# Layer 0 of a four-layer kernel: scores in two pairs of PSUM banks, weights normalised before they are turned, products on halved columns, one routing chain, broadcast norm factors

## The reference, cut to what matters

```
q, k, v = x @ wq.T (16 heads of 64), x @ wk.T, x @ wv.T (4 kv heads of 64)
q, k = rmsnorm(q), rmsnorm(k)
scores = q k^T / 8, masked to a causal window of 64
y = softmax(scores) @ v;  out = y @ wo.T
# beside it: layernorm, a small attention over the 4 batches, layernorm,
# router -> softmax -> top 2 of 8 experts, experts w1, gelu, w2
```

## Time and profile before

| | |
|---|---|
| median of three runs | 1451.62 us (1449.86, 1451.62, 1457.27) |
| the profiled execution, its own time | 1449.79 us |
| its span | 1448.0 us |
| mean granted TensorE clock | 0.926 of 2.4 GHz |
| busy, share of span: TensorE, VectorE, ScalarE, GpSimd | 89%, 63%, 46%, 21% |
| scores steps | 32, their maxima from 82.4 to 555.5 us |
| first GpSimd scatter of layer 0, of layer 1 | 182.80 us, 594.48 us |
| first exponential of layer 1 | 646.63 us |

### The profile page before, as it was taken

The page is one execution under the profiler, slowest core; times in us unless marked ns, Lnnn a source line. Parts: engine busy times, 40 slices in busy tenths (PEclk is TensorE's granted clock), DMA queues, the critical chain, the costliest instruction groups (busy, mean ns, idle before and its releaser), DMA issues.

```text
span 1448.0 us, 23894 instructions
## 1 busy us (share of the span) xinstructions
PE 1291.5 (89%) x9334; PEld 791.3 (55%) x9334; DVE 913.3 (63%) x1975; ACT 664.0 (46%) x1424; POOL 302.3 (21%) x309
## 2 busy tenths in 40 slices
PE   6878697997997888779899979999799989899998
PEld 4456565876674666445666757755344323224555
DVE  4478753343354568865687657677578868775366
ACT  2345042762651322016443535566466646576621
POOL 1242072000102510474001201044421312101000
PEclk8988698998998879759999989999999989999999
DMA  8000023332100220123523463321330121200000
GB/s 247 21 1 1 1 85 120 89 106 70 29 8 18 57 39 4 62 66 71 144 85 99 123 163 105 121 69 30 66 74 4 33 39 34 36 1 29 1 8 22
DMA packets 65101, 86.23 MB, mean 60 GB/s; under 512 B 9566, under 2 KB 49374, under 8 KB 63326
## 3 DMA queue, kind: packets, MB, share of 16 engines
q1 hardware_dynamic: 60892, 76.30, 20.1%
q0 software_dynamic: 4096, 8.40, 2.0%
HBM read 62.19 MB, written 22.48 MB: 58 GB/s over the span
## 4 chain that ended last, share of the span: by engine, by line
PE 63%; DVE 13%; DMA 9%; POOL 5%; issue 4%; ACT 3%; SPq 3%; DVEq 0%; ACTq 0%; POOLq 0%
PE psB L420 29%; PE psA L420 27%; PE psB L424 5%; DMA wA<-slots_x 3%; DVE mx L1478 2%; POOL slots_x L1945 2%; DMA arena<-scr1k 2%; PE psA L424 2%; DMA arena<-scr2k 2%; DVE st L1177 1%; ACT pbuf L1807 1%; ACT pbuf L1725 1%; DMA arena<-slots_x 1%; SPq L2049 1%; DMA scr1k<-arena 1%
## 5 line engine op out<-in xcount | busy, mean ns | idle before, releaser
L1807 ACT ACTIVATE pbuf<-psA 128x512 f32<-128x512 f32 (+3 forms) x768 | 350.6, 489 | 249.0 <-PE psA L420 241.1
L1478 DVE TENSOR_REDUCE mx<-psA 128x1 f32<-128x512 f32 (+3 forms) x520 | 326.0, 660 | 83.5 <-PE psA L420 80.7
L420 PE MATMUL psA<-arena 64*64 64x128 f32 (+6 forms) x1504 | 187.9, 291 | 2.2 <-ACT pbuf L1807 1.4
L420 PEld LDWEIGHTS psA<-arena 64*64 64x64 f32 (+3 forms) x1504 | 111.1, 135 | 70.4 <-ACT pbuf L1807 30.6
L1725 ACT ACTIVATE pbuf<-psA,st,rq 128x128 f32<-128x128 f32 x256 | 92.7, 467 | 99.9 <-DVE st L1181 99.9
L420 PE MATMUL psA<-arena,w 96*128 96x512 bf16 (+4 forms) x320 | 112.7, 404 | 6.1 <-DMA arena<-scr2k 3.3
L420 PE MATMUL psA<-w_mdiagT,w_identb 128*128 128x128 bf16 x512 | 108.8, 222 | 0.0
L420 PE MATMUL psB<-pbuf,arena 128*5 128x512 f32 (+3 forms) x1024 | 93.4, 438 | 0.5 <-ACT pbuf L1807 0.4
L420 PE MATMUL psB<-xf,wA 128*128 128x128 f32 x624 | 93.0, 294 | 0.0
L1904 POOL TENSOR_TENSOR sm<-sm,w_ohalf 128x4 f32<-128x4 f32 x24 | 24.5, 1030 | 294.7 <-DVE sm L1048 294.7
L420 PEld LDWEIGHTS psB<-xf,wA 128*128 128x128 f32 x624 | 81.5, 203 | 7.6 <-issue 2.4
(11 more groups left out here) (318 smaller groups left out, 2325.5 us busy)
## 6 DMA issues: line engine op xcount, KB each, us to landing
wA<-in_moe SPq DMA_DIRECT2D x39, 576.0 KB, 3.8
wA<-in_moe SPq DMA_DIRECT2D x39, 256.0 KB, 3.1
slots_x<-wA SPq DMA_DIRECT2D x20, 256.0 KB, 3.7
slots_y<-tH SPq DMA_DIRECT2D x18, 256.0 KB, 3.7
wA<-slots_x SPq DMA_DIRECT2D x15, 256.0 KB, 4.0
arena<-scr2k SPq DMA_DIRECT2D x48, 64.0 KB
scr1q<-arena SPq DMA_DIRECT2D x4, 384.0 KB, 3.9
scr1k<-arena SPq DMA_DIRECT2D x4, 384.0 KB, 4.2
```

The costliest lines, as they stand in the source:

```text
L420: return pe.matmul(out, lhsT, rhs, start=start, stop=stop, skip_group_check=True)
L1478: dv.tensor_reduce(m[:, t, h:h + c], maxb(lay, b, n)("mx", lay, b, n)[:, 0:c * k].rearrange("p (c k) -> p c k", c=c), AX.X, ALU.max) \
L1807: ac.activation(pb(lay, b, s, j)[:, 0:T - q0_], scoreb("ex", lay, b, s, j)[:, 0:T - q0_], ACT.Exp, bias=0.0, scale=1.0) \
```

## The change

- The scores alternate between two pairs of banks (psA0 and psA1). bT and outP go; turned tiles of both x and the products use accO alone, in turn. The output projection, and the first batch's ks0, rq0, kn0, use misc.
- The exponentials also give their row sums (accum_out). A new VectorE part nz inverts them and multiplies the weights in SBUF (128x512 per x) before they are turned. The column of ones goes.
- The products take v as the stationary side (64 columns, the left or right half of the output partitions) and the turned weights of both x as the moving side (128 columns), so their result is already turned; the four turns go, and the copy of yt is one plain copy. The heads' order in wo0 follows.
- ln3 and kn0 turn a broadcast view of the factors; the widening copies go.
- rt of layers 0 and 1 is a copy of the logits per batch; a new step rts does softmax and comparisons for all four batches at once, in instructions of 128x1024.
- MERGE is written anew. In it, layer 0's routing stands before the first batch's sixth scores step (before: its seventh), the scatter steps still before the second batch's ks0, and the fourth batch's k0, ks0 and kn0 among the third batch's steps (before: behind them), so that they also stand ahead of the second gather as they did.

The diff, cut to its core (MERGE, renamed signals and lines that only follow are left out):

```diff
-        both = Ring([A[0][:, :, :]])
+        both = Ring([a[:, :, :] for a in A])
         scoreb = Ring([A[0][:, k, :] for k in range(2)])
-        bT = Ring([A[1][:, 1, :]])
-        outP = Ring([A[1][:, 0, :]])
...
-        PTs = Ring([v.rearrange("p (k c) -> p k c", k=4) for v in ptiles[4:7]])
-        ysb = Ring([ptiles[7].rearrange("p (k x d) -> p k x d", k=4, x=2)])
+        PTs = Ring([pbuf[:, i, :, :].rearrange("p x (k c) -> p x k c", k=4) for i in (2, 3)])
...
-                pe.wait_ge(*ln_wide.at(tag, b))
-                v, bank = tA("wide", tag, b).rearrange("p (t r) -> p t r", t=4), misc(*u)
-                tr4(bank, lambda t: v[:, t, :]).then_inc(*ln_turned.up(tag, b))
-                tA.give(("wide", tag, b), ln_turned.now())
+                pe.wait_ge(*ln_pow.at(tag, b))
+                st, bank = small("ln", tag, b), misc(*u)
+                tr4(bank, lambda t: st[:, 4 + t:5 + t].to_broadcast([P, P])).then_inc(*ln_turned.up(tag, b))
+                small.give(("ln", tag, b), ln_turned.now())
...
-                    pe.wait_ge(*w)
-                pe.wait_ge(*kn_wide.at(b, kv))
-                v = tQ(*u).rearrange("p (t r) -> p t r", t=4)
-                tr4(nr(b)(*u), lambda t: v[:, t, :]).then_inc(*kn_turned.up(b, kv))
-                tQ.give(u, kn_turned.now())
+                for w in misc.free(*u):
+                    pe.wait_ge(*w)
+                pe.wait_ge(*ks_pow.at(b))
+                st = smq("ks", b)
+                tr4(misc(*u), lambda t: st[:, 16 + 4 * kv + t:17 + 4 * kv + t].to_broadcast([P, P])).then_inc(*kn_turned.up(b, kv))
...
-                for w in bT.free(*u):
-                    pe.wait_ge(*w)
-                pe.wait_ge(*s_exp.at(b, i, x))
-                pt, sm = bT(*u), Sm(b, i, x)
+                for w in accO.free(*u):
+                    pe.wait_ge(*w)
+                pe.wait_ge(*s_n.at(b, i, x))
+                pt, sm = accO(*u), Sm(b, i, x)
                 for k in range(4):
                     m = tr(pt[:, k * P:k * P + P], sm[:, k, :])
...
-            def yv(b, i, x):
+            def yv(b, i):
                 kv, h = windows(i)
-                for w in outP.free(b, i, x):
-                    pe.wait_ge(*w)
-                pe.wait_ge(*(p_sba if x else p_sbv).at(b, i))
-                pe.wait_ge(*v_sb.at(b, 3))
-                ps, bank = PTs(b, i, x), outP(b, i, x)
-                for k in range(4):
-                    m = mm(bank[:, 65 * k:65 * k + 65], ps[:, k, :], vwin[b % 2][:, 4 * h + k, kv, :], True, True)
-                m.then_inc(*y_mm.up(b, i, x))
-                PTs.give((b, i, x), y_mm.now())
-
-            def yt(b, i):
                 u = "yT", b, i
                 for w in accO.free(*u):
                     pe.wait_ge(*w)
-                pe.wait_ge(*y_n.at(b, i, 1))
-                y = ysb(b, i)
+                pe.wait_ge(*p_sbv.at(b, i))
+                pe.wait_ge(*p_sba.at(b, i))
+                pe.wait_ge(*v_sb.at(b, 3))
+                ps, bank = PTs(b, i), accO(*u).rearrange("p (x k i) -> p x k i", x=2, k=4)
                 for k in range(4):
-                    m = tr(accO(*u)[:, P * k:P * k + P], y[:, k, :, :].rearrange("p x d -> p (x d)"))
-                m.then_inc(*y_tr.up(b, i))
-                ysb.give((b, i), y_tr.now())
+                    for hf in range(2):
+                        r = slice(64 * hf, 64 * hf + 64)
+                        m = mm(bank[r, :, k, :], vwin[b % 2][:, 4 * h + k, kv, :], ps[:, :, k, r], True, True)
+                m.then_inc(*y_mm.up(b, i))
+                PTs.give((b, i), y_mm.now())
             def wo0(b, h):
                 u = "wo", b, h
-                for w in bT.free(*u):
+                for w in misc.free(*u):
                     pe.wait_ge(*w)
                 pe.wait_ge(*y_sb.at(b, 4 * h + 3))
                 for p in range(4 * h, 4 * h + 4):
                     kv = p // 2
                     y = qsb[b % 2][:, 2 * kv:2 * kv + 2, :].rearrange("p h (a c) -> p a h c", a=2)[:, p % 2]
-                    m = mm(bT(*u).rearrange("p (h c) -> p h c", h=2), W["wo0"][:, p, :], y, p == 4 * h, p == 4 * h + 3)
+                    m = mm(misc(*u).rearrange("p (h c) -> p h c", h=2), W["wo0"][:, p, :], y, p == 4 * h, p == 4 * h + 3)
...
-                dv.tensor_copy(tQ("kn", b, kv).rearrange("p (t r) -> p t r", t=4),
-                               st[:, 16 + 4 * kv:20 + 4 * kv].unsqueeze(2).to_broadcast([P, 4, P])).then_inc(*kn_wide.up(b, kv))
...
+            def nz(b, i, x):
                 u = b, i, x
                 for w in rcp.free(*u):
                     dv.wait_ge(*w)
-                y4 = outP(*u)[:, 0:260].rearrange("p (a d) -> p a d", a=4)
-                dv.wait_ge(*y_mm.at(*u))
-                dv.reciprocal(rcp(*u), y4[:, :, 64]).then_inc(*y_rc.up(*u))
-                for w in ysb.free(b, i):
-                    dv.wait_ge(*w)
-                dv.wait_ge(*y_rc.at(*u))
-                dv.tensor_tensor(ysb(b, i)[:, :, x, :], y4[:, :, 0:64], rcp(*u).unsqueeze(2).to_broadcast([P, 4, 64]), ALU.mult) \
-                    .then_inc(*y_n.up(*u))
-                outP.give(u, y_n.now())
-                rcp.give(u, y_n.now())
+                dv.wait_ge(*s_exp.at(*u))
+                dv.reciprocal(rcp(*u), st2(b, i)[:, 4 * x:4 * x + 4]).then_inc(*s_rc.up(*u))
+                if x:
+                    st2.give((b, i), s_rc.now())
+                dv.wait_ge(*s_rc.at(*u))
+                dv.tensor_tensor(Sm(*u), Sm(*u), rcp(*u).unsqueeze(2).to_broadcast([P, 4, P]), ALU.mult).then_inc(*s_n.up(*u))
+                rcp.give(u, s_n.now())
+
+            def tp(b, i, x):
+                if x == 0:
+                    for w in PTs.free(b, i):
+                        dv.wait_ge(*w)
+                    dv.wait_ge(*p_tr.at(b, i, x))
+                    dv.tensor_copy(PTs(b, i)[:, 0].rearrange("p k c -> p (k c)"), accO("pt", b, i, x)).then_inc(*p_sbv.up(b, i))
+                    accO.give(("pt", b, i, x), p_sbv.now())
...
+                tmp = route[:, 2:4]
+                for w in small.free("sx", lay) + tF.free("rk", lay) + tF.free("rk2", lay):
...
+                softmax(lg, small("sx", lay), 16, (lay,))
+                small.give(("sx", lay), vstep.now())
+                pj = lg.unsqueeze(2).to_broadcast([P, 16, 8, 8])
+                pe_ = lg.unsqueeze(3).to_broadcast([P, 16, 8, 8])
+                dv.wait_ge(*vstep.now())
+                dv.tensor_tensor(rk, pj, pe_, ALU.is_equal).then_inc(*vstep.up())
+                dv.tensor_tensor(rk2, pj, pe_, ALU.is_gt).then_inc(*vstep.up())
+                dv.wait_ge(*vstep.now())
+                dv.tensor_tensor(rk, rk, W["tril8"][:, 0:8, :].unsqueeze(1).to_broadcast([P, 16, 8, 8]), ALU.mult).then_inc(*vstep.up())
+                dv.wait_ge(*vstep.now())
+                dv.tensor_tensor(rk, rk, rk2, ALU.add).then_inc(*vstep.up())
+                tF.give(("rk2", lay), vstep.now())
+                dv.wait_ge(*vstep.now())
+                dv.tensor_reduce(r3, rk, AX.X, ALU.add).then_inc(*vstep.up())
...
+                dv.tensor_tensor(top_b[:, 0:16, :], top_m[:, 0], top_m[:, 1], ALU.add).then_inc(*rt_out.up(lay))
...
+                dv.wait_ge(*rt_mm.at(lay, b))
+                bank = misc("lg", lay, b)[:, 0:32].rearrange("p (t e) -> p t e", e=8)
+                if lay < 2:
+                    dv.tensor_copy(route[:, 0, 4 * b:4 * b + 4, :], bank).then_inc(*rt_in_sb.up(lay, b))
+                    misc.give(("lg", lay, b), rt_in_sb.now())
...
                         a = ac.activation(sm[:, k, :], S[:, x, P * k:P * k + P], ACT.Exp, bias=st[:, 8 + 4 * x + k:9 + 4 * x + k],
-                                          scale=rq(b)[:, 4 * h + k, kv, x:x + 1])
+                                          scale=rq(b)[:, 4 * h + k, kv, x:x + 1], accum_out=st[:, 4 * x + k:4 * x + k + 1])
...
-                    ac.activation(PTs(b, i, x).rearrange("p k c -> p (k c)"), bT("pt", b, i, x), ACT.Copy, scale=1.0).then_inc(*p_sba.up(b, i))
-                    bT.give(("pt", b, i, x), p_sba.now())
+                    ac.activation(PTs(b, i)[:, 1].rearrange("p k c -> p (k c)"), accO("pt", b, i, x), ACT.Copy, scale=1.0).then_inc(*p_sba.up(b, i))
...
+                ac.wait_ge(*y_mm.at(b, i))
                 ac.wait_ge(*s_mm.at(b, 2 * kv + 1))
-                ac.activation(qsb[b % 2][:, 2 * kv + h, :].rearrange("p (a k i) -> p k a i", a=2, i=64),
-                              accO("yT", b, i).rearrange("p (k a i) -> p k a i", a=2, i=64), ACT.Copy, scale=1.0).then_inc(*y_sb.up(b, i))
+                ac.activation(qsb[b % 2][:, 2 * kv + h, :], accO("yT", b, i), ACT.Copy, scale=1.0).then_inc(*y_sb.up(b, i))
...
-                ffn += [("rt", lay, b) for b in four] + [("dsp", lay)] + [("xt", lay, b) for b in four]
+                ffn += [("rt", lay, b) for b in four] + [("rts", lay), ("dsp", lay)] + [("xt", lay, b) for b in four]
...
-                for i in range(10):
```

(8 more changed lines are left out.)

239 lines of the change are left out of this document (97 added, 142 removed).

## The result

The changed kernel takes **1436.06 us** (median of 4 runs, 1432.73 to 1440.69) where the kernel before takes 1450.82: a ratio of 0.9891, with a 95% interval of 0.9851 to 0.9931. It is 14.8 us faster; 45 had been forecast. The profiled execution is of 1435.45 us, span 1433.6.

What follows compares the result with a forecast made beforehand. It took layer 0 as bound by a staircase of hand-overs, TensorE 48% of its chain, and the tail by TensorE at 93%. Stage terms summed to -46: 1449.8 - 46 + 1.8 = 1405.6, so 1406 us; range 1376 to 1450.

Steps and rivals of the forecast that it cites:

- Before the first scatter: Start to first scatter: -4 us (0 to -8) from shorter norm loops up to 82.4 us, then -15 up to 182.8.
- VectorE's stage: 82.4 to 182.8 us, VectorE fullest: routing -10, second norm -4, one moved scores step -3.3, wider normalising +2.5; -15 together.
- Products: Layer 0's scores steps: 16 passes with 64 stationary columns take 1.07 us, saving TensorE 1.6 us a step.
- Rival B: Layer 0's products: loads as wide as now, or halves one after the other; +19 us, 1425 us; chance 12%.
- Sums: Layer 0's 256 exponentials also give row sums: 0.13 us each on ScalarE, 1.0 us a step.
- rival A: ScalarE becomes the bound: row sums cost 0.34 us each, a second-batch step 8.1 us; 1420 us; chance 14%.
- The failing step between the scatters: First to second scatter: key loop -4, second batch's stage -3, third's -14, fourth's -6; 27 us expected.
- the key loop's -4: 182.8 to 248.7 us: scatter unchanged, the key norms' loop after it shorter without widening copies; -4 us (+3 to -8).
- 6.2 to 7.1 us apart: Sign that the forecast is right: spacing of scores maxima in batches two and three, not 7.4 us.
- The failing step of the tail: 594.5 us to the end, after the second scatter: eight widening copies go, order rewritten with the same work; 0 (-8 to +12).
- Rival C: Layer 0's shared bank: products and turns wait for copies behind ScalarE's exponentials; steps about 10 us, 1471 us; chance 11%.
- Rival D: No gain: after 182.8 us waits move, 27 us not had, 15 lost to new waits in 24 steps; 1448 us; chance 9%.

## Why the prediction was wrong in size

The kernel became faster and the time lies in the stated range, but only a third of the forecast gain came (14.8 of 45 us), and the forecast's own value was 30 us low. By its steps:

*Before the first scatter* (-19, measured -24.8) the path was right and the sum low: the first norms gave 9.4 us, not 4, since the 9 us by which their loops were to shorten passed on whole. VectorE's stage gave 15.3 with 15 forecast, partly by luck: on the slower chips norms and routing gave 11.2 of it (14 forecast) and attention 4.1 (1 forecast).

*Products* (1.07 us a step): right, 1.09 at clock 1.00. Rival B fell by its price. The Trainium skill (TensorEngine Tiling (Array Packing), Restrictions) says that column tiling disables Fast Weight Load; it gives no price, and the prediction's reading of it, products near 2.0 us, is not borne out. Whether the loads of either kernel were fast ones no run here shows.

*Sums* (0.13 each): 0.08, and rival A fell twice: by the price, and by the 4.2 us, if any, that all of them cost. What the Trainium skill (VectorE: DVE Perf Modes, Two Vector instructions with no wait between them) says of VectorE, that an accumulator output is two instructions, the rows above show for ScalarE too; they overlap with the next activation.

*The failing step between the scatters* is the passing from work to time: the terms -4, -3, -14 and -6, 27 us, measured 5.6. The stage sum let TensorE's savings through almost whole, though the prediction's own first part had said that layer 0 is a staircase and that TensorE holds 48% of its chain. 24.1 us of TensorE's work went there; at the measured rate of a fifth to 0.3 they are worth 5 to 7. The other two engines' time passed on no better: a quarter of VectorE's 28.3 us with the multiplication. Normalising "in the second batch it fits (VectorE 3.5 of 7.4)" was right: 1.3 us in that whole batch. It was dear where VectorE is the fullest engine, 1.5 us a step ahead of the first scatter, and there the forecast had only the difference to the old multiplications, +2.5. What kept the change positive is the item for which no separate number was given: without the second pair it is 30 us slower. (These prices are of single edits to the changed kernel; they do not add up to the change, since the kernel before multiplied and turned too.)

By stages: the key loop's -4 became +2.2. The second batch's key power starts 24.3 us earlier (198.93 us, not 223.27), right behind the last scatter in both kernels; but behind it TensorE first does the turns and products that the first batch's last steps left over, and experts, and is hardly idle up to the next scores. The steps that "6.2 to 7.1 us apart" was to show are 10.1 apart, because more of the other work, the fourth batch's keys too, stands between them; the gap from the third's last maximum to the fourth's first is 29.1 us, as forecast (under 35). Within the third batch's stage the two moves work against each other: that gap shrank by 22.4 us, and the third batch's seven steps grew by 15.2. The 7.4 itself was mis-divided: eight maxima bound seven steps, so the 59.00 us of the earlier trace rows are 8.4 each. In the fourth batch's stage TensorE's wait for the routing of layer 1 is 8.4 us, 4.2 before, with +4 forecast; beside it stands the wait of 8.2 us for the stack, of which the cost is open.

*The failing step of the tail* is "the order is rewritten with the same work in the same proportions: 0 (-8 to +12)". It grew by 16.0, and putting the old order back takes off 11.7 and 12.0. The proportions were not the same: 30 exponentials more stand before layer 1's last expert, and the gap comes back as idle time plus a lower clock. On the slower chip this is all of it (from the second scatter to the end 919.7 us with the old tail, 919.4 in the kernel with norms and routing alone); on the faster one the old tail's stretch is still 7 us longer in one profile than before (860.5, not 853.5), and this rest stays open.

*Rival C* was wrong for this kernel and right about the mechanism: the old order, in which turns wait for the copy out of the shared bank, costs 97 us. One of its signs is met, steps above 9 us (10.1), the other is not: turns wait 4.7 us for that copy between the scatters. The order was costed at nothing in layer 0 as well; it is what makes the edit work. *Rival D* (1448) had the nearest reading of what follows the first scatter: about 21 of the 27 us were not had, and 16 more were lost, but in the tail rather than in 24 steps. Its own sign, the second scatter at 590, is not met: it stands at 564.0, where the stage sum would have put it near 548.

**A version that beats both**: the changed kernel with the old order from layer 1's first exponentials on, 1422.9 us, 11.7 under the changed kernel and 2.0% (1.6 to 2.5) under the kernel before.

## What to carry to other kernels

In a stretch where several engines hand over to each other and none is full, do not let an engine's saved time through whole: here a fifth to 0.3 of TensorE's and a quarter of VectorE's showed. In a stretch where one engine is the fullest and holds the chain, its time counts whole or more: the same multiplication cost 1.5 us a step there and 0.25 elsewhere. A second buffer that lets a step start before the last one is read out can be worth more than all the work taken out: here 30 us. When a change comes with a rewritten order, count how much independent work still stands beside each transfer or short chain that the fullest engine must wait out, as spent filler returns as idle time and then as a lower clock. Test order and code crossed, and test both halves of an order together, since each half alone can show nothing. And before a test of a wait, see that the wait is there in the run beside it.

## What the runs showed of the hardware

The same kernel takes 1434.6 us on one chip and 1545.7 on another. Up to the first scatter both profiles agree within 0.2 us (158.4 us in both). Then the slower one has single stalls, the first of them between the first scatter and the second batch, whose stretch is 96 us there and 68 here. The waits in it (slower chip):

```profile
DVE st L1149 <- remote: 19.1, 1, 19.1
PE psA L415 <- issue: 18.3, 9, 2.4
DVE xT L1005 <- remote: 17.5, 1, 17.5
```

In the profiles of the changed kernel on the faster chips no wait of that stretch is put down to "remote". The chain of waits of the slower one has 7% of the span under "another core or an unknown queue", about 108 us, nearly all of the difference of 111. What these releasers are, the profile does not name, and no run tried it; the kernel before takes 8% longer on these chips too, and the changed kernel's ratio held (0.9865 on both).

The second surprise is what idle time can cost behind itself: ten microseconds with 3.3 us of it are followed by ten at clock 0.59, in which the same eight passes take 1.9 us instead of 1.0. In the tail, busy time and idle time of the changed kernel exceed the old order's by about the same, 7.1 and 6.4 us.
